# Two-layer kernel with a Hadamard weight stage: first stage of seven gate and up groups on GpSimd, mixer splits placed in the second chunk

## The chip, the cores and the metric

The kernel runs on one core of one Trainium2 chip. The metric is the device time of one execution in microseconds (us). TensorE is called PE below, VectorE DVE, ScalarE ACT, GpSimd POOL, and SyncE, which only issues DMAs here, SP.

## What is computed

Two layers over 2048 tokens of width 512, each with a token mixer and a feed-forward part, all with a residual sum after a layer norm:

```python
x = x + scan_layer(layernorm(x))        # selective scan, 16 states, over time
x = x + ffn(layernorm(x))               # fwht(x*SU_ug), W_up, W_gate, silu, fwht(.*SU_dp), W_down
x = x + mixer(layernorm(x))             # x,z = split(h@W_in.T); x@conv_w.T; (x*D)*silu(z) @ W_out.T
x = x + moe(layernorm(x))               # 64 experts, top 8, capacity 128
```

`fwht` is the Walsh-Hadamard transform. Since it is linear, the kernel applies it to the weights: the transform over the 512 rows of a gate or up weight is a 4 by 4 Hadamard matrix over row blocks of 128, times a 128 by 128 one inside a block. In the mixer the product of `conv_w` and the x half of `W_in` is made once from the weights (the fold). All weights are stored to a scratch tensor in memory as a high and a low part, so that three fast products of rounded numbers stand for one exact one.

## The kernel before

**Tiling and stages.** The 2048 tokens are four chunks of 512. For each chunk the scan runs over 16 states n, and the code divides each state into four positions m = 0 to 3; a position is numbered `state_at(c, n, m)` = 5 + 64c + 4n + m. Every engine walks the same positions in the same order, each with its own program, and does at a position what tables (`prep_at`, `fold_at`, `plain_at`, `quanta_at`) place there. After the four chunks comes a drain, the routing of tokens, and a loop over the 64 experts.

**The scan of a state.** On DVE, state n is: `bx` = u times the broadcast row B_n (L1265), two scans (L1274), two more scans, and `hc` = bx times the broadcast row C_n (L1292); between these DVE does the side work of positions m = 0, 1, 2 and 3. PE makes the broadcasts (`bcast_b` L660, `bcast_c` L668), ACT the decays (L938), and POOL adds `hc` to `y` (L1450, called add(n) below). `bcast_c(n)` waits for hc(n-1); hc(n) waits for `bcast_c(n)` and for add(n-1); in states where the bank of C is lent to other work (`borrowed`), `bcast_c(n)` stands behind the side work of position m = 2.

**The weight stage in chunk 0.** `kinds` = "uduuuduuduud" lists twelve groups, u for 512 columns of the gate or up weight, d for 128 columns of the down weight; group i has four places, 3 + 4i to 6 + 4i, so the stage fills states 0 to 11, one group per state, shifted by two positions. Place (i, m) is on PE four fp32 products (L630, `prep`), on ACT one rounding to the high part at the next position (`prep_hi` L869, L872), on DVE the low part (`prep_lo` L1154, L1159), and on SP two stores (`store_prep`). The raw weights sit in `raw_u`, which has two buffers, and in `raw_d`, which has one. For a d group POOL multiplies the raw block by a scale (L1470) and makes two stages of the transform (L1480, `butterfly`); PE's place (i, 0) of a d group waits for the last of them. The tables put the three parts of the butterfly of the second d group (index g = 1) into states 2, 3 and 4, those of g = 2 at (6,1), (6,3) and (7,1), those of g = 3 at (9,0), (9,1) and (10,0). They are called b(g,0), b(g,1), b(g,2) here.

**The fold and the plain splits.** The fold is eight places, four from position (13,1) of chunk 0 and four from (1,0) of chunk 1. PE multiplies (L642), ACT and DVE split into `fst` (L876, L1166), SP stores. The plain splits are sixteen tiles of `W_in` (z half) and `W_out`, which are only split and stored: SP loads into `praw`, ACT rounds (`plain_hi`, L876), POOL subtracts (`plain_lo`, L1486), SP stores `fst`. `fst` has two buffers; the ACT step of tile i waits for the stores of tile i-2 (`S_ms`). They stand at every third position from (0,2) of chunk 0. The first products of the feed-forward part, read from a ring of six buffers (`load_ring`), start at position (3,0) of chunk 1.

**Queues.** Each engine has one program order, which is also the order of its waits. On POOL, within a position, the side work (`gated_lo`) comes first, then `plain_lo`, then the norm, the corrections of the softplus (L1493, L1495, in states 9 and 10 at m = 3) and the butterflies; add(n) is last in state n.

## Time and profile before

| | us |
|---|---|
| median of 3 runs | 1742.09 (1740.38 to 1750.31) |
| profiled execution | 1734.25 |
| its span on the core | 1732.4 |
| PE busy | 1503.9 (87%) |
| DVE busy | 1062.3 (61%) |
| ACT busy | 586.8 (34%) |
| POOL busy | 794.1 (46%) |
| chunk 0, from bx(0) to bx(0) of chunk 1 | 45.0 to 281.2 |
| chunk 1, likewise | 281.2 to 520.0 |

The page's busy shares are means over stages with different limits. A record of PE includes time in which the next product already runs, so a row of eight products that spans 3.60 us is the better measure of their rate than the mean of one; and each fp32 product of the code is two records. In a timeline row the bracket at the end is the idle time before the row on its engine, and what ended it.

### The profile page before, as it was taken

How to read it: one execution, taken by the hardware profiler on the slowest of the kernel's cores; microseconds unless marked ns; L12 is line 12 of the kernel's file. 1: busy time of each engine (PE TensorE's matmuls, PEld its weight loads, DVE VectorE, ACT ScalarE, POOL GpSimd, SP SyncE). 2: the span in 40 equal slices, each digit the busy share in tenths (PEclk: the TensorE clock that was granted, in tenths of full speed). 3: DMA queues.
4: the chain of work that ended last, by engine and by line, in shares of the span. 5: the costliest groups of instructions: out<-in, count | busy, mean ns of one | idle time of the engine just before them, and what ended most of it. 6: DMA issues, size and time to landing. Idle time of an engine off the chain costs nothing. (4 is left out here: it accounts for less than half of the span.)

```text
span 1732.4 us, 19079 instructions
## 1 busy us (share of the span) xinstructions
PE 1503.9 (87%) x5792; PEld 1032.0 (60%) x5792; DVE 1062.3 (61%) x1591; ACT 586.8 (34%) x1034; POOL 794.1 (46%) x491
## 2 busy tenths in 40 slices
PE   6989966899948899988999899999992799999992
PEld 3344323577736677766887787778772455555551
DVE  4887688787898887889988755452453122222220
ACT  4444633344534335343423322121210122222220
POOL 3467853353644445634554325662276222222222
PEclk9999988999969999999999999999995899999996
DMA  6899663356644666657555568997760699999986
GB/s 203 255 279 279 195 221 130 97 160 196 202 142 149 200 218 219 218 170 245 189 183 167 150 200 275 374 322 233 233 204 25 184 314 312 323 321 322 322 227 126
DMA packets 193541, 380.41 MB, mean 220 GB/s; under 512 B 20994, under 2 KB 95106, under 8 KB 192944
## 3 DMA queue, kind: packets, MB, share of 16 engines
q1 hardware_dynamic: 164784, 321.71, 58.2%
q0 software_dynamic: 20032, 39.92, 9.7%
q10 hardware_dynamic: 8640, 17.73, 2.9%
q8 instruction: 42, 0.69, 0.2%
q14 instruction: 43, 0.35, 0.1%
HBM read 301.65 MB, written 124.35 MB: 246 GB/s over the span
## 5 line engine op out<-in xcount | busy, mean ns | idle before, releaser
L1450 POOL TENSOR_TENSOR y<-y,hc 128x2048 f32<-128x2048 f32 x64 | 293.2, 4581 | 249.0 <-DVE hc L1292 249.0
L588 PE MATMUL bank<-tokT,ring 128*128 128x512 f32 x768 | 307.3, 400 | 12.8 <-DVE xall L1147 6.9
L1274 DVE TENSOR_TENSOR_SCAN bx<-bank,state,bx 128x512 f32<-128x512 f32 x256 | 312.7, 1267 | 0.8
L590 PE MATMUL bank<-tokT,ring 128*128 128x512 f32 x768 | 302.0, 393 | 0.0
L589 PE MATMUL bank<-tokT,ring 128*128 128x512 f32 x768 | 301.7, 393 | 0.0
L938 ACT ACTIVATE bank<-dl,an 128x512 f32<-128x512 f32 x256 | 171.0, 684 | 329.6 <-DVE bx L1274 329.5
L1456 POOL TENSOR_TENSOR act<-th,act 128x512 fp32r<-128x512 f32 x96 | 126.3, 1315 | 269.0 <-ACT act L862 268.7
L817 PE MATMUL bank<-wgu,xeT 128*128 128x384 f32 x512 | 177.7, 490 | 0.0
L588 PEld LDWEIGHTS bank<-tokT,ring 128*128 128x128 f32 x768 | 145.7, 190 | 49.0 <-issue 17.4
L600 PE MATMUL bank<-ring,act 128*128 128x512 f32 x360 | 147.6, 410 | 22.7 <-DVE th L1136 17.4
L590 PEld LDWEIGHTS bank<-tokT,ring 128*128 128x128 f32 x768 | 145.6, 190 | 32.0
L589 PEld LDWEIGHTS bank<-tokT,ring 128*128 128x128 f32 x768 | 145.9, 190 | 29.4
L1292 DVE TENSOR_TENSOR hc<-bx,bank 128x2048 f32<-128x2048 f32 x64 | 146.0, 2282 | 24.4 <-PE bank L668 23.7
L1265 DVE TENSOR_TENSOR bx<-u,bank 128x2048 f32<-128x2048 f32 x64 | 146.0, 2282 | 9.4 <-PE bank L660 6.3
L602 PE MATMUL bank<-ring,act 128*128 128x512 f32 x360 | 143.4, 398 | 0.0
L601 PE MATMUL bank<-ring,act 128*128 128x512 f32 x360 | 143.3, 398 | 0.0
L1532 POOL DMA_INDIRECT slots<-row,idx x128 | 126.2, 986 | 36.9 <-issue 33.5
L1129 DVE SCALAR_TENSOR_TENSOR th<-th,bank 128x512 f32<-128x512 f32 x96 | 65.7, 684 | 100.1 <-ACT th L857 99.9
L817 PEld LDWEIGHTS bank<-wgu,xeT 128*128 128x128 f32 x512 | 93.2, 192 | 52.1 <-issue 2.0
L834 PE MATMUL bank<-wde,hT 96*128 96x512 f32 x256 | 120.6, 593 | 0.5 <-DVE hT L1432 0.5
L1422 DVE SCALAR_TENSOR_TENSOR te<-te,bank 128x192 f32<-128x192 f32 x64 | 22.7, 355 | 156.9 <-ACT te L1078 156.9
L630 PE MATMUL bank<-raw_u,had 128*128 128x512 f32 x256 | 113.7, 594 | 0.2 <-DMA raw_u<-wgT_in 0.2
(147 smaller groups left out, 2032.3 us busy)
## 6 DMA issues: line engine op xcount, KB each, us to landing
ring<-w_all SPq DMA_DIRECT2D x288, 512.0 KB, 3.7
wgu<-wgu_in SPq DMA_DIRECT2D x64, 768.0 KB, 7.6
wde<-wd_in SPq DMA_DIRECT2D x64, 384.0 KB, 6.1
slots<-empty_in SPq DMA_DIRECT2D x16, 1154.0 KB, 8.2
xe<-slots ACTq DMA_DIRECT2D x60, 288.5 KB, 7.1
w_all<-staged_u SPq DMA_DIRECT2D x64, 256.0 KB, 3.2
w_all<-fst SPq DMA_DIRECT2D x48, 256.0 KB, 3.7
w_all<-staged_d SPq DMA_DIRECT2D x32, 256.0 KB, 4.0
```

The lines of the kernel that those rows point to most:

```text
L588: nc.tensor.matmul(b[:, :], w[:, k, 0, :], x[:, 0, k, :], start=(k == 0), stop=False)
L589: nc.tensor.matmul(b[:, :], w[:, k, 0, :], x[:, 1, k, :], start=False, stop=False)
L590: last = nc.tensor.matmul(b[:, :], w[:, k, 1, :], x[:, 0, k, :], start=False, stop=(k == KT - 1))
L600: nc.tensor.matmul(PF[t][:, :], act8[:, 0, j, tok], w[:, 0, :], start=(j == 0), stop=False)
L601: nc.tensor.matmul(PF[t][:, :], act8[:, 0, j, tok], w[:, 1, :], start=False, stop=False)
L602: last = nc.tensor.matmul(PF[t][:, :], act8[:, 1, j, tok], w[:, 0, :], start=False, stop=(j == pairs - 1))
L817: last = nc.tensor.matmul(CG[i % 2][:, 0:2 * FE], xeT[:, i % 2, k, :], wgu[i][:, k, :], start=(k == 0), stop=(k == KT - 1))
L938: nc.scalar.activation(dA[k % 2][:, :], dl[c % 2][:, k, :], ACT.Exp, scale=an[:, k, n:n + 1]).then_inc(S_dA, 1)
L1265: nc.vector.tensor_tensor(bx[:, :, :], u[:, :, :], PB[:, :].unsqueeze(1).to_broadcast([P, KT, CH]), ALU.mult).then_inc(S_bm, 1)
L1274: nc.vector.tensor_tensor_scan(bx[:, k, :], dA[k % 2][:, :], bx[:, k, :], state[:, k, n:n + 1], ALU.mult, ALU.add).then_inc(S_sc, 1)
L1292: nc.vector.tensor_tensor(hc[:, :, :], bx[:, :, :], PC[:, :].unsqueeze(1).to_broadcast([P, KT, CH]), ALU.mult).then_inc(S_cm, 1)
L1450: nc.gpsimd.tensor_tensor(y[c % 2][:, :, :], y[c % 2][:, :, :], hc[:, :, :], ALU.add).then_inc(S_ya, 1)
```

## The change

Three edits. **Pair sums.** For the seven u groups behind the first, POOL makes block 0 + block 2 and block 1 + block 3 (part 0), and the two differences (part 1), into a new buffer `paired`; each part is one instruction of 128 x 1024. PE then needs two products for a place in place of four. Part 0 of group i stands on POOL at the position of place 4i - 2 of the list, which is m = 0 of state i - 1, and part 1 at m = 2 of it. PE waits for the part that it reads (`S_pd`); a part waits for the products that read the same half of `paired` last. **Raw loads.** A buffer of `raw_u` is loaded again after place m = 1 of its group and not after m = 3. **Plain splits.** They stand behind the fold, at every second position from (3,2) of chunk 1 to (11,0), and the numbering of `fst` changes to fit. The sixteen loads and thirty-two stores of SP move with them.

```diff
--- before.py
+++ after.py
@@ -156,6 +156,7 @@
                 raw_d = sb(prep_only, "raw_d", [P, 2, M0 * P])
                 wsdp = sb(prep_only, "wsdp", [P, D])
                 had = sb(prep_only, "had", [P, 2, P])
+                paired = sb(prep_only, "paired", [P, 2, 2, 512])
             rawd, sums = raw_d[:, 0, :], raw_d[:, 1, :]
             ring = sb(A, "ring", [P, RING, 2 * D], f32r)
             expert_buffers((4,))
@@ -209,7 +210,7 @@
             S_x = [sem(f"x_in{c}") for c in range(NCH)]; S_id = sem("identity_in"); S_w = sem("weights_in")
             S_raw = [sem("raw_in0"), sem("raw_in1")]; S_rawd = sem("raw_down_in")
             S_wsc = sem("raw_scaled"); S_pmm = sem("prep_mm"); S_ph = sem("prep_hi"); S_pl = sem("prep_lo")
-            S_bf = sem("butterfly"); S_sel = sem("selectors")
+            S_bf = sem("butterfly"); S_pd = sem("pairs_summed"); S_sel = sem("selectors")
             S_su = [sem(f"up_stored{i}") for i in range(4)]; S_sd = [sem(f"down_stored{i}") for i in range(2)]
             S_wx = sem("winx_in"); S_cv = sem("conv_in"); S_pr = [sem(f"plain_in{i}") for i in range(4)]
             S_fm = sem("fold_mm"); S_mh = sem("mixer_hi"); S_fl = sem("fold_lo"); S_wl = sem("plain_lo")
@@ -272,9 +273,11 @@
             group_of = [kinds[:i].count(kinds[i]) for i in range(len(kinds))]
             prep_places = list(range(3, 3 + 4 * len(kinds)))
             prep_at = {place: (i // 4, i % 4) for i, place in enumerate(prep_places)}
+            u_at = [i for i, kind in enumerate(kinds) if kind == "u"]
+            pairs_at = {prep_places[4 * i - 2 + 2 * part]: (i, part) for i in u_at[1:] for part in range(2)}
             fold_at = {state_at(0, 13, 1) + 3 * m: (0, m) for m in range(KT)} | {state_at(1, 1, 0) + 2 * m: (1, m) for m in range(KT)}
             FOLDS, PLAINS = 2 * KT, 2 * M1
-            plain_at = {state_at(0, 0, 2) + 3 * i: i for i in range(PLAINS)}
+            plain_at = {state_at(1, 3, 2) + 2 * i: i for i in range(PLAINS)}
 
             borrowed_b, borrowed_c = {}, {}
             for c in range(NCH):
@@ -386,16 +389,16 @@
                     def store_mixer(i):
 
                         s = i % 2
-                        if i < M1 or i >= PLAINS:
-                            which = 0 if i < M1 else 1
-                            f = i if i < M1 else i - PLAINS
+                        if i < FOLDS + M1:
+                            which = 1 if i < FOLDS else 0
+                            f = i if i < FOLDS else i - FOLDS
                             m, half = f % KT, f // KT
                             t0 = M0 + 4 * half
                             for part in range(2):
                                 dst = gate_up[which, t0:t0 + 4, :, m, part, :].rearrange("t p c -> p t c")
                                 sp.dma_start(dst, fst[:, s, part, :].rearrange("p (t c) -> p t c", t=4).bitcast(fp32)).then_inc(S_ms[s], 16)
                         else:
-                            j = i - M1
+                            j = i - FOLDS - M1
                             for part in range(2):
                                 sp.dma_start(a["w_all"][3 * (M0 + j) + 2, :, D * part:D * part + D],
                                              fst[:, s, part, :].bitcast(fp32)).then_inc(S_ms[s], 16)
@@ -442,8 +445,11 @@
                             i, m = prep_at[pos - 2]
                             store_prep(i, m)
                             g = group_of[i] + (2 if kinds[i] == "u" else 1)
-                            if m == 3 and g < kinds.count(kinds[i]):
-                                sp.wait_ge(S_pmm, 4 * i + 4)
+                            if m == (1 if kinds[i] == "u" and group_of[i] else 3) and g < kinds.count(kinds[i]):
+                                if kinds[i] == "u" and group_of[i]:
+                                    sp.wait_ge(S_pd, 2 * group_of[i])
+                                else:
+                                    sp.wait_ge(S_pmm, 4 * i + 4)
                                 load_raw(kinds[i], g)
                             if (i, m) == (len(kinds) - 1, 3):
                                 sp.wait_ge(S_pmm, 4 * len(kinds))
@@ -452,7 +458,7 @@
                         if pos - 2 in fold_at:
                             half, m = fold_at[pos - 2]
                             sp.wait_ge(S_fl, KT * half + m + 1)
-                            store_mixer(PLAINS + KT * half + m)
+                            store_mixer(KT * half + m)
                             if half == 0 and m == KT - 1:
                                 load_conv(1)
 
@@ -473,13 +479,13 @@
                                 sp.dma_start(chunk(acc[0], c), xall[:, c]).then_inc(S_x3, 16)
 
                     def plain(pos):
-                        if pos == state_at(0, 0, 0):
+                        if pos == state_at(1, 1, 0):
                             for i in range(4):
                                 load_plain(i)
                         if pos - 3 in plain_at:
                             i = plain_at[pos - 3]
                             sp.wait_ge(S_wl, i + 1)
-                            store_mixer(i)
+                            store_mixer(FOLDS + i)
                             if i + 4 < PLAINS:
                                 load_plain(i + 4)
 
@@ -620,10 +626,19 @@
                     def prep(i, m):
                         g = group_of[i]
                         if kinds[i] == "u":
-                            pe.wait_ge(S_raw[g % 2], 16 * (g // 2 + 1))
+                            if g == 0:
+                                pe.wait_ge(S_raw[0], 16)
+                            else:
+                                pe.wait_ge(S_pd, 2 * (g - 1) + m // 2 + 1)
                         else:
                             pe.wait_ge(S_bf, 4 * g + 4)
                         wait(pe, S_pl, 4 * (i - 1) + m + 1)
+                        if kinds[i] == "u" and g:
+                            for k in range(2):
+                                last = nc.tensor.matmul(PF[m][:, :], had[:, k * (m % 2), :], paired[:, m // 2, k, :],
+                                                        start=(k == 0), stop=(k == 1))
+                            last.then_inc(S_pmm, 1)
+                            return
                         for k in range(4):
                             x = raw_u[:, g % 2, k, :] if kinds[i] == "u" else \
                                 rawd.rearrange("p (x m h) -> p x m h", x=4, m=4)[:, :, k, :]
@@ -877,7 +892,7 @@
 
                     def plain_hi(i):
                         act.wait_ge(S_pr[i % 4], 16 * (i // 4 + 1))
-                        mixer_hi(i, praw[:, i % 4, :])
+                        mixer_hi(FOLDS + i, praw[:, i % 4, :])
 
                     def side(pos):
                         if pos in plain_at:
@@ -887,7 +902,7 @@
                         if pos - 1 in fold_at:
                             half, m = fold_at[pos - 1]
                             act.wait_ge(S_fm, KT * half + m + 1)
-                            mixer_hi(PLAINS + KT * half + m, PF[m][:, :])
+                            mixer_hi(KT * half + m, PF[m][:, :])
                         for h, kind, j in quanta_at.get(pos - 2, ()):
                             if kind == "up":
                                 gated_hi(h, j)
@@ -1161,8 +1176,8 @@
 
                     def fold_lo(half, m):
                         i = KT * half + m
-                        dve.wait_ge(S_mh, PLAINS + i + 1)
-                        dve.wait_ge(S_ms[i % 2], 32 * ((PLAINS + i) // 2))
+                        dve.wait_ge(S_mh, i + 1)
+                        wait(dve, S_ms[i % 2], 32 * (i // 2))
                         nc.vector.tensor_tensor(fst[:, i % 2, 1, :], PF[m][:, :], fst[:, i % 2, 0, :].bitcast(fp32),
                                                 ALU.subtract).then_inc(S_fl, 1)
 
@@ -1480,11 +1495,20 @@
                             nc.gpsimd.tensor_tensor(qv[:, :, i, :], pv[:, :, 0, :], pv[:, :, 1, :], op).then_inc(S_bf, 1)
 
                     def plain_lo(i):
-                        pool.wait_ge(S_mh, i + 1)
+                        pool.wait_ge(S_mh, FOLDS + i + 1)
                         s = i % 2
-                        wait(pool, S_ms[s], 32 * (i // 2))
+                        pool.wait_ge(S_ms[s], 32 * ((FOLDS + i) // 2))
                         nc.gpsimd.tensor_tensor(fst[:, s, 1, :], praw[:, i % 4, :], fst[:, s, 0, :].bitcast(fp32),
                                                 ALU.subtract).then_inc(S_wl, 1)
+
+                    def pair_sums(i, part):
+
+                        g = group_of[i]
+                        pool.wait_ge(S_raw[g % 2], 16 * (g // 2 + 1))
+                        if g > 1:
+                            pool.wait_ge(S_pmm, 4 * u_at[g - 1] + 2 * part + 2)
+                        nc.gpsimd.tensor_tensor(paired[:, part, :, :], raw_u[:, g % 2, 0:2, :], raw_u[:, g % 2, 2:4, :],
+                                                ALU.subtract if part else ALU.add).then_inc(S_pd, 1)
 
                     def correction(c, k):
 
@@ -1505,6 +1529,8 @@
                                 side(state_at(c, n, m))
                                 if state_at(c, n, m) - 1 in plain_at:
                                     plain_lo(plain_at[state_at(c, n, m) - 1])
+                                if state_at(c, n, m) in pairs_at:
+                                    pair_sums(*pairs_at[state_at(c, n, m)])
                                 if c >= 1 and (n, m) == (1, 2):
                                     norm_rstd(pool, n2, c - 1)
                                 if c >= 1 and (n, m) == (14, 0):
```

## Rows read from the trace of the kernel before

**Rows 1.** Groups by shape, 0 to 480 us: busy, mean ns, idle before.
```profile
L630 PE MATMUL bank<-raw_u,had 128*128 128x512 f32 x256 | 113.7, 594 | 0.2 <-DMA raw_u<-wgT_in 0.2
...
L1480 POOL TENSOR_TENSOR raw_d<-raw_d 128x1024 f32<-128x1024 f32 x16 | 37.5, 2365 | 0.2
...
L1486 POOL TENSOR_TENSOR fst<-praw,fst 128x512 fp32r<-128x512 f32 x16 | 20.3, 1270 | 23.4 <-ACT fst L876 23.4
...
L876 ACT ACTIVATE fst<-praw 128x512 fp32r<-128x512 f32 x16 | 9.9, 619 | 0.0
```

**Rows 2.** Windows of states 2, 6, 7 and 10: length, busy by engine, PE clock, DMA.
```profile
core 0: us, PE busy (x) PEld busy (x) DVE busy (x) ACT busy (x) POOL busy (x), PEclk, DMA share, GB/s
...
73.06:86.30 13.24, 13.24 (x34) 5.97 (x33) 11.82 (x11) 5.67 (x10) 10.29 (x4) 1.00 1.06 301
...
133.34:148.26 14.92, 14.92 (x43) 7.28 (x42) 11.93 (x11) 6.87 (x12) 14.92 (x6) 1.00 1.02 294
148.26:165.83 17.57, 17.57 (x43) 7.97 (x42) 12.56 (x12) 7.44 (x13) 11.30 (x6) 1.00 0.86 257
...
196.84:217.58 20.74, 17.67 (x38) 7.41 (x37) 11.98 (x11) 12.19 (x21) 18.89 (x12) 0.92 0.44 132
```

**Rows 3.** Timeline of DVE, chunk 0: start, length, instruction, idle before and releaser.
```profile
79.79 0.75 DVE L1154 SCALAR_TENSOR_TENSOR staged_u<-bank,vec,staged_u 128x512 fp32r<-128x512 f32 x1 [1.42 <-ACT staged_u L869]
...
130.33 2.29 DVE L1292 TENSOR_TENSOR hc<-bx,bank 128x2048 f32<-128x2048 f32 x1 [0.78 <-PE bank L668]
...
163.03 2.29 DVE L1292 TENSOR_TENSOR hc<-bx,bank 128x2048 f32<-128x2048 f32 x1 [1.14 <-PE bank L668]
...
214.77 2.29 DVE L1292 TENSOR_TENSOR hc<-bx,bank 128x2048 f32<-128x2048 f32 x1 [3.28 <-PE bank L668]
```

**Rows 4.** Timeline of PE, chunk 0, the d groups' first places and the fold.
```profile
159.16 3.60 PE L630 MATMUL bank<-raw_d,had 128*128 128x512 f32 x8
162.19 0.80 PE L668 MATMUL bank<-xdr,sel 128*128 128x512 f32 x1
...
209.20 5.31 PE L630 MATMUL bank<-raw_d,had 128*128 128x512 f32 x8 [3.07 <-POOL raw_d L1480]
213.94 0.80 PE L668 MATMUL bank<-xdr,sel 128*128 128x512 f32 x1
...
243.69 8.56 PE L642 MATMUL bank<-conv,winx 128*128 128x512 f32 x16 [3.13 <-DMA winx<-winx_in]
```

**Rows 5.** Windows behind PE's idle time at 206 us, same columns as rows 2.
```profile
209.20:212.20 3.00, 3.00 (x4) 1.45 (x5) 2.10 (x3) 2.76 (x6) 2.92 (x3) 0.50 0.63 176
212.20:215.20 3.00, 3.00 (x8) 1.38 (x8) 0.43 (x1) 0.66 (x2) 2.92 (x3) 0.96 0.61 175
```

**Rows 6.** Timeline of POOL, chunk 0, from hc(5) and from hc(8).
```profile
132.70 4.53 POOL L1450 TENSOR_TENSOR y<-y,hc 128x2048 f32<-128x2048 f32 x1 [10.09 <-DVE hc L1292]
...
138.42 4.52 POOL L1470 TENSOR_TENSOR raw_d<-raw_d,wsdp 128x2048 f32<-128x2048 f32 x1
...
144.12 4.69 POOL L1480 TENSOR_TENSOR raw_d<-raw_d 128x1024 f32<-128x1024 f32 x2
148.78 4.51 POOL L1450 TENSOR_TENSOR y<-y,hc 128x2048 f32<-128x2048 f32 x1
153.25 4.64 POOL L1480 TENSOR_TENSOR raw_d<-raw_d 128x1024 f32<-128x1024 f32 x2
...
178.33 4.54 POOL L1450 TENSOR_TENSOR y<-y,hc 128x2048 f32<-128x2048 f32 x1 [7.17 <-DVE hc L1292]
...
204.49 4.66 POOL L1480 TENSOR_TENSOR raw_d<-raw_d 128x1024 f32<-128x1024 f32 x2
```

**Rows 7.** Timeline of DVE and POOL, chunk 1, states 9 to 11.
```profile
429.77 0.69 DVE L1129 SCALAR_TENSOR_TENSOR th<-th,bank 128x512 f32<-128x512 f32 x1 [5.02 <-ACT th L857]
...
456.31 4.58 POOL L1450 TENSOR_TENSOR y<-y,hc 128x2048 f32<-128x2048 f32 x1
...
461.91 2.28 DVE L1292 TENSOR_TENSOR hc<-bx,bank 128x2048 f32<-128x2048 f32 x1
```

**Rows 8.** The page's DMA issues: count, KB each, us to landing.
```profile
w_all<-fst SPq DMA_DIRECT2D x48, 256.0 KB, 3.7
```

## The prediction

> **What bounds the kernel now.** I read the windows of each scan state in chunk 0, since both edits lie in chunks 0 and 1; then the timeline of DVE, which carries the scan, for what ends each of its waits; then PE and POOL at the places found. The windows show PE full in states 2, 6 and 7, and DVE busy for about 12 us in each [rows 2]. A full PE looks like the bound, but is not in most states: state 2 lasts 13.24 us, which is DVE's 11.8 us and one wait of 1.42 us, ended by ACT's rounding, which stands behind the fourth decay in ACT's program [rows 3]. More speed on PE takes nothing from that. PE ends a wait of DVE by itself in only a few places: 0.78 us at hc(5), 1.14 us at hc(7) [rows 3], about 0.6 us at hc(6), and some 3 us in front of the low parts of states 7 and 9. One wait that looks like PE's is POOL's: hc(10) waits 3.28 us for a broadcast [rows 3], which stands behind the first place of a d group, and this place had waited 3.07 us for POOL's last butterfly [rows 4]. POOL has no idle time in state 6 and 18.9 us of 20.7 in state 10 [rows 2]. So from state 5 to state 10 PE and POOL are nearly level behind DVE, and the change moves work from one to the other.
>
> **Part 1, what PE loses.** Seven groups of four places lose two products each, 56 in all, each of them two records. Eight records take 3.43 us from start to start (the row's 3.60 us less the overlap; the same is seen for u places), or 0.43 us each [rows 4], so PE loses 112 x 0.43 = 48 us of work; the mean of 594 ns in the grouped row would make it 67 us, but that mean counts overlap twice [rows 1]. A u place then takes 1.7 us and a u state 7.5 us of PE. Nearly all of this turns into idle time of PE, for DVE's 13.2 us stay.
>
> **Part 2, what POOL gets.** Fourteen sums of 128 x 1024. The nearest row is the butterfly of the same shape, 2365 ns, from start to start 2.34 us [rows 1, 6]: 33 us more. The sixteen plain subtractions of 1270 ns, 20 us, leave chunk 0 [rows 1]. The net is +13 us on POOL, and what matters is where. Two chains, each from an hc to the last butterfly of a d group, decide.
>
> First chain, from hc(5)'s end. Before: add(5) starts at 132.70, and b(2,2) ends at 157.87 (153.25 and two of 2.3) [rows 6], 25.2 us later, with two plain subtractions of 1.24 us in it. PE came to the place that reads this only at 159.16 [rows 4], 26.5 us after 132.70, and hc(7) could start at 163.03 [rows 3]. After: the two subtractions leave (-2.5), and pair sums (7,0) and (7,1) come in (+4.7), one ahead of b(2,0) and one ahead of b(2,1). The chain is then 27.4 us. No wait sits inside it: hc(6) ends well before add(6) comes up, and the raw blocks land earlier than now. So the place starts 0.9 us later relative to hc(5), although PE by then could have been there some 6 us sooner. And it starts with a cold PE: behind the idle time at 206 us the granted clock was 0.50, the 1.2 GHz level, for 3 us, then 0.96 [rows 5], and the eight records and the broadcast behind them took 4.74 us (209.20 to 213.94) where at the full clock they took 3.03 us (159.16 to 162.19) [rows 4]. That is +1.7 us. Bounds of this one: 0 if the clock stays up, 3.0 us if all eight records run at half speed.
>
> What comes ahead of it: the wait of 0.78 us at hc(5) goes, because the u place before that broadcast is 1.7 us shorter; state 4 loses one plain rounding on ACT that stood ahead of the rounding DVE waits for, 0.6 us [rows 1]; but b(1,2) ends 1.1 us later (the pair sums of states 2 and 3 put add(3) back by that), of which I count 0.7 us at DVE. Net -0.7 us at hc(5). So hc(7) is at -0.7 + 0.9 + 1.7 = +1.9 us.
>
> Second chain, from hc(8)'s end. Before: 178.33 to the end of b(3,2) at 209.15 [rows 6], with two subtractions (2.5 us) and 0.3 us of waiting for a raw block in it. After: pair sums (10,0) and (10,1), +4.7 us. Net +1.9 us; PE starts cold here already before, so nothing is added for the clock. In state 9 DVE would win 0.5 us (PE earlier) and 0.6 us (the rounding gone from ACT), but hc(10) is set by POOL, so both are swallowed. hc(10) stands at 1.9 + 1.9 = **+3.8 us**. States 8 and 11 keep their length: their d places are not changed, and the waits in them are for DVE, ACT and the stores of the two `staged_d` buffers. States 0 to 3 keep theirs as well: pair sums that come late there hold PE, not DVE, for hc needs a place two positions old.
>
> **Part 3, raw loads and DMA in chunk 0.** The earlier reload adds no wait: SP's wait for `S_pd`, with the stores of `staged_u` queued behind it, is met before the low part that SP has just waited for. Leaving out 12 MB of plain traffic relieves a queue that is full in state 2 (share 1.06) and 6 (1.02) [rows 2]. DVE waits for no DMA directly; what can gain is the start of the fold, where PE waits 3.13 us for `winx` [rows 4]. Bounds 0 and -3.1 us; I take -0.5 us, near zero, as the plain stores issued around it are queued behind that load.
>
> **Part 4, plain splits in chunk 1.** Sixteen ACT roundings (0.62 us), sixteen POOL subtractions (1.27 us) [rows 1], 16 loads, 32 stores. All hidden behind 10 us and more per state in which ACT waits for DVE, with these exceptions: at (9,2) ACT is late, DVE waits 5.02 us for its tanh [rows 7], and the rounding stands ahead of it: +0.6 us. In state 10 one subtraction stands ahead of the corrections and add(10): add(10) ends at 460.9 and hc(11) starts at 461.91 [rows 7], a slack of 1.0 us, against 1.27 us: +0.3 us. Each rounding waits for the stores of the tile two before; the spacing of two positions leaves one position (about 3.3 us) between their issue by SP and the wait, where it was three, and the landing takes 3.7 us [rows 8] and SP 1 us for the two. ACT reaches the (n,0) ones about 4.5 us and the (n,2) ones about 7 us behind the issue, by the order of its program, so I count 0, bound 1.5 us a state in eight states. SP's wait for the subtraction has ring loads behind it; the ring holds six loads, so this costs nothing unless SP is late by over 10 us. In sum +0.9 us.
>
> **Sum.** 3.8 - 0.5 + 0.9 = +4.2 us. Against the profiled execution's 1734.25 us that is 1738.4 us; the profiled execution lies 7.8 us under the median of the runs, so against the median of 1742.09 it is **1746.3 us**.
>
> **Rivals.**
> A, the relief of PE counts. If POOL is not late (pair sums cheaper, or PE's arrival the real limit where I see POOL), then hc(5) -0.8, hc(6) -0.6, state 7 about -4.7 (158.3 where hc(7) now starts at 163.03), state 9 -1.1 and part of the 3.3 us at hc(10): -8 to -10 us, 1733 us. For it: PE is full in states 6 and 7. Against it: the row of the same shape on POOL, and POOL's own full state 6 [rows 2, 6].
>
> B, slower by ACT's wait for `fst` in chunk 1. From the point at which a pair of stores takes over some 4.5 us from issue to landing, ACT stands at the plain rounding with the tanh behind it, and DVE waits for that. The price is the excess, 1.5 us in each of eight states, 12 us with both buffers in phase: 1742.1 + 3.3 + 12 = 1757 us. For it: 3.7 us is a median, with ring loads and 1.1 MB fills in the same queue. Against it: the (n,2) tiles have slack, and chunk 1's DMA share is about a half.
>
> C, PE stays cold. PE idles 5 us in most u states after the change. If the clock does not come back within the first d place, then places (8,1) to (8,3), which fill state 8 without slack, take 3.4 us more each: +10 us beyond the sum, 1756 us. For it: the clock stood at 0.50 for 3 us after one idle stretch; against it: it came back at once [rows 5]. The Trainium skill, TensorE: Matmul & The Clock Gate, in "HAM oscillation", says that a kernel whose matmul bursts are parted by idle gaps falls back to the low clock in each gap and pays for the warm-up again each time. By that rule the term of 1.7 us at hc(7) is right and C is its repetition; the trace agrees in one place, with 4.74 against 3.03 us.
>
> D, no effect: the pair sums just fill POOL and DVE hides all, 1742 us. This needs the first chain to end before PE comes, 0.9 us less than I count.
>
> **Chances.** Forecast (between +1 and +8 us) 0.45; D and near it 0.17; A 0.14; B 0.14; C 0.10. A measurement of this kernel can tell about 0.5%, 8.7 us, from no change. Under 1733.4: most of A, 0.13. Above 1750.8: B, C and a little of the forecast's upper end, 0.25. Within: 0.62. The range for 8 in 10 leaves out the outer half of A and the outer part of B and C: 1734 to 1757 us.
>
> **What would show it.** L630 on `raw_u` at 144 records; L630 on `raw_d` at 159 us to start on POOL, with some 6 us of idle time, and at granted clock 0.5; hc(7) to wait about 6 us for L668; bx(8) about 1.9 us and bx(11) about 3.8 us later than 165.83 and 217.58; PE busy in chunk 0 down by 50 us or more; chunk 1 within 1 us of its 238.7 us. I am wrong if hc(7) starts before 163 us (then A), if ACT's L876 waits for the stores of `fst` in chunk 1 (then B), or if the windows of states 8 and 9 show the clock near 0.5 (then C).

## The result, and the profile after

| | before, on the same chip | after |
|---|---|---|
| median (lowest to highest) | 1745.13 (1740.38 to 1750.31) | 1776.84 (1770.84 to 1781.55) |
| profiled execution | 1734.25 | 1777.88 |
| span | 1732.4 | 1776.0 |
| chunk 0, bx(0) to bx(0) of chunk 1 | 236.3 | 241.7 |
| chunk 1, likewise | 238.7 | 259.1 |

The ratio is 1.0173, 95% interval 1.0144 to 1.0202. The forecast, 1746.3 with 1734 to 1757 as its range, is wrong. The change costs 31.7 us by the medians. The two profiled executions lie 43.6 us apart, since that of before is 10.9 us under its median and that of after 1.0 us above. To find where the time went, I took the start of `bx` of every state from both traces. The last state of chunk 3 starts 29.4 us later: +5.6 at the end of chunk 0, +20.4 in chunk 1, +3.4 in chunks 2 and 3. The other 14.2 of the 43.6 us lie behind that state. That stretch is the same program in all kernels here and took 751.5 us (before) to 765.7 us (after) in the thirteen traces, and 761.9 in that of before with idle products, which has nothing of the change; so I don't count it to the change. Of the executions behind the medians below, one of the twelve of "five groups, idle products" took 5800.27 us at a mean granted clock of 0.258; its median counts it, its ratio does not.

First the line of busy times on the page of after. POOL was at 794.1 us before and PE at 1503.9.

```profile
PE 1482.6 (83%) x5680; PEld 1019.6 (57%) x5680; DVE 1063.4 (60%) x1591; ACT 587.0 (33%) x1034; POOL 826.3 (47%) x505
```

PE has the 112 records less that were counted, and POOL the 14 more. Then the groups by form of the first 520 us of after (busy us and mean ns, then idle us ahead of them and what ended most of it), to hold against [rows 1].

```profile
L638 PE MATMUL bank<-paired,had 128*128 128x512 f32 x112 | 59.3, 660 | 24.7 <-POOL paired L1510 24.7
L1510 POOL TENSOR_TENSOR paired<-raw_u 128x1024 f32<-128x1024 f32 x14 | 32.9, 2359 | 0.0
L891 ACT ACTIVATE fst<-praw 128x512 fp32r<-128x512 f32 x16 | 10.0, 626 | 40.7 <-DMA w_all<-fst 40.6
```

The pair sum costs 2359 ns, as the butterfly of the same shape did. The third line is the result: sixteen roundings of 626 ns, and ahead of them ACT stood idle for 40.6 us waiting for stores of `fst`. Now the windows of chunk 0, chunk 1, and two of 3 us at the first place of the second last d group (start:end and length, busy us of each engine, granted clock, DMA share, GB/s).

```profile
45.20:286.89 241.69, 172.76 (x378) 73.97 (x376) 188.74 (x158) 101.50 (x172) 158.55 (x57) 0.89 0.60 179
286.89:545.94 259.05, 206.43 (x762) 147.44 (x763) 200.58 (x182) 108.19 (x185) 130.79 (x67) 0.88 0.61 192
160.16:163.16 3.00, 3.00 (x4) 1.45 (x5) 0.00 (x0) 0.00 (x0) 0.00 (x0) 0.51 0.62 173
163.16:166.16 3.00, 3.00 (x8) 1.35 (x8) 0.33 (x1) 0.57 (x1) 0.00 (x0) 0.92 0.00 0
```

In chunk 1 DVE, which carries the scan, is busy for 200.6 of 259.1 us, against 199.0 of 238.7 before. Its work has hardly grown; its waits have.

**Chunk 1.** The view of waits of after, in 287 to 546 us (us in total, times, longest):

```profile
ACT fst L891 <- DMA w_all<-fst: 40.6, 7, 11.3
DVE th L1144 <- ACT th L872: 32.9, 10, 8.6
```

and of before, in 281 to 520 us:

```profile
DVE th L1129 <- ACT th L857: 16.0, 6, 5.3
```

DVE's waits for the tanh grew by 16.9 us, and this is most of the chunk's 20.4. One place shows the mechanism, the rounding of plain tile 10, which needs the buffer of tile 8. Timelines of after around 420 us, SP, then POOL (the low part of tile 8), ACT (the rounding of tile 10 and the tanh) and DVE (start, us, engine, line, in brackets the idle time and what ended it):

```profile
410.73 0.98 SPq L399 DMA_DIRECT2D w_all<-fst  x2
413.57 5.76 SPq L425 DMA_DIRECT2D ring<-w_all  x3
419.38 0.64 SPq L414 DMA_DIRECT2D slots<-empty_in  x1
420.07 1.10 SPq L403 DMA_DIRECT2D w_all<-fst  x2
```

```profile
409.10 1.30 POOL L1501 TENSOR_TENSOR fst<-praw,fst 128x512 fp32r<-128x512 f32 x1 [5.23 <-ACT fst L891]
```

```profile
429.97 0.63 ACT L891 ACTIVATE fst<-praw 128x512 fp32r<-128x512 f32 x1 [11.32 <-DMA w_all<-fst]
430.50 0.67 ACT L872 ACTIVATE th<-bank,gsh 128x512 f32<-128x512 f32 x1
```

```profile
431.21 0.69 DVE L1144 SCALAR_TENSOR_TENSOR th<-th,bank 128x512 f32<-128x512 f32 x1 [8.60 <-ACT th L872]
```

POOL ends the low part of tile 8 at 410.4. SP first issues the stores of tile 7 (410.73), three ring loads, for which it waits for PE, and a fill of 1154 KB; the pair of tile 8 it issues at 420.07, 9.7 us behind the low part. ACT came to the rounding at 418.65 (429.97 less 11.32 us of waiting), so 1.4 us before the stores were even issued, and gets the buffer back at 429.97, 8.8 us behind the end of the issue and 9.9 behind its start. The tanh of L872 is next in ACT's program, and DVE is idle for 8.60 us until it has it. The other six waits have the same two parts: SP issues 1.3 to 9.2 us behind the low part, and ACT has the buffer 5.4 to 9.8 us behind the issue. The DMA view of 410 to 432 us says what the stores were among (count, KB each, median us from issue to landing):

```profile
q1 hardware_dynamic: 3175, 6.27, 94.0%
w_all<-fst SPq DMA_DIRECT2D x7, 256.0 KB, 7.8
slots<-empty_in SPq DMA_DIRECT2D x1, 1154.0 KB, 9.7
```

The queue takes 94.0% of sixteen engines' time in this stretch, and a store lands after 7.8 us, where the median over the whole kernel of before was 3.7 [rows 8]. In the kernel before, the same work with its fill, but without the plain tiles, took 69.9% (405 to 427 us):

```profile
q1 hardware_dynamic: 1535, 4.85, 69.9%
```

**Chunk 0.** DVE's timeline at hc(7) and hc(10) of after, to hold against [rows 3]:

```profile
165.83 2.29 DVE L1307 TENSOR_TENSOR hc<-bx,bank 128x2048 f32<-128x2048 f32 x1 [6.62 <-PE bank L683]
...
219.96 2.29 DVE L1307 TENSOR_TENSOR hc<-bx,bank 128x2048 f32<-128x2048 f32 x1 [6.77 <-PE bank L683]
```

PE's, to hold against [rows 4]:

```profile
160.16 5.40 PE L645 MATMUL bank<-raw_d,had 128*128 128x512 f32 x8 [4.87 <-POOL raw_d L1495]
164.99 0.80 PE L683 MATMUL bank<-xdr,sel 128*128 128x512 f32 x1
...
213.77 5.91 PE L645 MATMUL bank<-raw_d,had 128*128 128x512 f32 x8 [5.97 <-POOL raw_d L1495]
219.12 0.80 PE L683 MATMUL bank<-xdr,sel 128*128 128x512 f32 x1
```

And POOL's, the first chain, to hold against [rows 6]:

```profile
132.75 4.54 POOL L1465 TENSOR_TENSOR y<-y,hc 128x2048 f32<-128x2048 f32 x1 [6.22 <-DVE hc L1307]
137.25 2.34 POOL L1510 TENSOR_TENSOR paired<-raw_u 128x1024 f32<-128x1024 f32 x1
139.55 4.54 POOL L1485 TENSOR_TENSOR raw_d<-raw_d,wsdp 128x2048 f32<-128x2048 f32 x1
144.03 2.38 POOL L1510 TENSOR_TENSOR paired<-raw_u 128x1024 f32<-128x1024 f32 x1
146.35 4.69 POOL L1495 TENSOR_TENSOR raw_d<-raw_d 128x1024 f32<-128x1024 f32 x2
150.98 4.53 POOL L1465 TENSOR_TENSOR y<-y,hc 128x2048 f32<-128x2048 f32 x1
155.44 4.66 POOL L1495 TENSOR_TENSOR raw_d<-raw_d 128x1024 f32<-128x1024 f32 x2
```

From 132.75 to 160.1 POOL has no gap. PE waited 4.87 us for the last butterfly, and then its clock stood at 0.51, the 1.2 GHz level, for 3 us, before it was 0.92 (the windows above). The eight records and the start of the broadcast took 4.83 us, where they took 3.03 us at the full clock [rows 4].

### The profile page after: what moved, and what is told of

Same layout as the page of the kernel before. It is cut to its first block and busy times, and to the rows that moved or that the text cites. A ratio compares the mean times of both kernels' runs of the same rounds, so it can differ in the third digit from the quotient of the medians.

```text
span 1776.0 us, 18881 instructions
## 1 busy us (share of the span) xinstructions
PE 1482.6 (83%) x5680; PEld 1019.6 (57%) x5680; DVE 1063.4 (60%) x1591; ACT 587.0 (33%) x1034; POOL 826.3 (47%) x505
## 5 line engine op out<-in xcount | busy, mean ns | idle before, releaser
L1592 POOL DMA_INDIRECT out<-ye,tok x32 | 49.3, 1541 | 141.2 <-ACT ye L1100 124.1
```

## The experiments

The theory after this result: chunk 1 is lost to ACT's wait for the stores of `fst`, which land late for two reasons, a queue shared with ring loads and fills, and an SP that comes to the stores late; chunk 0 is lost to POOL's two chains and PE's low clock behind each. The rivals: chunk 1 is lost because the added ACT and POOL work is itself too much there; the two parts of the change need each other; the pair sums are slow at all seven groups, not in the two chains. Each table row below gives how much later (us) than in the trace of before a state's `bx` starts. A row is one execution. After, fills later, and fills later with early stores run the same code in chunk 0 and differ there by up to 0.4 us, so I read nothing into less than that; the execution of five groups is the slowest of its ten, 9.4 us above its median.

| kernel | (0,5) | (0,8) | (0,11) | (1,0) | (1,7) | (1,11) | (2,0) | (3,15) |
|---|---|---|---|---|---|---|---|---|
| after | 1.0 | 2.8 | 5.2 | 5.6 | 9.9 | 24.0 | 26.0 | 29.4 |
| pairs only | 5.4 | 9.6 | 15.0 | 15.7 | 15.9 | 15.9 | 15.9 | 19.2 |
| plains only | 0.2 | 0.5 | -0.5 | -0.2 | 4.1 | 17.2 | 17.5 | 20.9 |
| four `fst` | 2.2 | 4.0 | 6.4 | 6.9 | 7.6 | 8.1 | 10.1 | 10.6 |
| fills later | 1.0 | 2.8 | 5.2 | 5.5 | 8.4 | 14.5 | 16.7 | 22.6 |
| fills later, stores early | 1.4 | 3.2 | 5.6 | 5.9 | 6.4 | 7.8 | 10.1 | 16.3 |
| five groups | 1.2 | -2.1 | -1.9 | -1.4 | 2.5 | 3.0 | 3.3 | 9.1 |
| idle products | 0.5 | -0.4 | 2.3 | 2.8 | 3.5 | 4.0 | 5.9 | 7.2 |
| sums on DVE | 0.2 | 3.3 | 4.3 | 6.0 | 10.0 | 10.5 | 10.8 | 10.9 |
| five groups, plains back | 4.9 | 2.9 | 2.8 | 3.1 | 3.0 | 3.0 | 3.0 | 3.1 |
| five groups, idle products | 0.2 | -3.8 | -6.5 | -6.3 | -6.0 | -5.4 | -5.1 | -2.6 |
| before with idle products | 0.4 | -0.8 | -2.8 | -2.5 | -2.4 | -2.4 | -2.4 | -2.0 |

Before had a median of 1745.13 beside after; of 1737.26 beside pairs only, plains only, four `fst` and fills later; of 1742.41 beside five groups, idle products, sums on DVE, and five groups with the plains back; and of 1737.28 beside the other three.

### One part of the change at a time

**Pair sums alone.** The plain splits stay at their old places in chunk 0. From after:

```diff
-            plain_at = {state_at(1, 3, 2) + 2 * i: i for i in range(PLAINS)}
+            plain_at = {state_at(0, 0, 2) + 3 * i: i for i in range(PLAINS)}
```

> The pair sums and the earlier raw loads alone; the plain splits stay in chunk 0 as before. Theory now (two parts: POOL's chains in chunk 0 cost about 5 us, ACT's waits for the stores of fst in chunk 1 cost about 20 us): with the plain subtractions still on POOL, each of the two chains is 2.5 us longer than in the changed kernel, so chunk 0 ends 9 to 10 us later than in the kernel before, chunks 1 to 3 keep the lengths of before, and the time is before + 8 to 11 us. Rival (it is the pair sums that disturb what comes later, through POOL and the reads of raw blocks): chunk 1 is longer by 10 us or more here too, and the time is before + 25 us or more.

Measured: 1756.20 us, ratio 1.0087 (1.0048 to 1.0126). Chunk 1 lost 0.2 us, chunk 0 lost 15.7. The chains account for what was expected, but 5.4 us are gone already at state 5, which no theory had. Of these, 4.5 are lost in state 3. POOL and DVE at its end in this run, then in the kernel before:

```profile
104.45 4.54 POOL L1465 TENSOR_TENSOR y<-y,hc 128x2048 f32<-128x2048 f32 x1
104.59 4.48 DVE L1132 TENSOR_SCALAR n_ngt<-n_mvt 128x4 f32<-128x4 f32 x1
```

```profile
99.08 4.53 POOL L1450 TENSOR_TENSOR y<-y,hc 128x2048 f32<-128x2048 f32 x1 [1.63 <-DVE hc L1292]
102.56 1.08 DVE L1117 TENSOR_SCALAR n_ngt<-n_mvt 128x4 f32<-128x4 f32 x1
```

POOL is full in states 2 and 3 with plain subtractions and pair sums together, and add(3) starts at 104.45 in place of 99.08. DVE pays for that in two ways. A u place comes late on PE, and DVE waits 1.0 us for its rounding. The other 3.4 us are in a tiny instruction of the layer norm, `n_ngt` (128 x 4), which takes 0.17 us where POOL is idle (570.03 us in after). It took 1.08 us before, 1.94 after and 4.48 here, and each time it ended within 0.1 us of the end of POOL's add(3): it stood until POOL's instruction was done. So POOL can take the plain subtractions or the pair sums, but not both in chunk 0; moving the plain splits saves 10.1 us there (15.7 against 5.6).

**Plain splits moved, alone.** From after, the four products of each place, the old raw waits, and no pair sums:

```diff
-            pairs_at = {prep_places[4 * i - 2 + 2 * part]: (i, part) for i in u_at[1:] for part in range(2)}
+            pairs_at = {}
```

> The move of the plain splits alone; PE keeps four products for each place. Theory: chunk 0 is 1 to 3 us shorter than before (the ACT roundings are gone from DVE's way, PE still sets hc(7)), chunk 1 is 18 to 22 us longer, with ACT's L891-kind wait for the stores of fst at about 40 us in sum; time before + 17 to 23 us. Rival (the two parts disturb each other): chunk 1 is longer by less than 10 us here.

Measured: 1760.68 us, ratio 1.0133 (1.0092 to 1.0174); chunk 0 -0.2 us, chunk 1 +17.7. The view of waits of chunk 1 of this run:

```profile
ACT fst L878 <- DMA w_all<-fst: 38.8, 7, 9.7
```

Chunk 1's loss comes with the plain splits and needs nothing of the pair sums. The freed time in chunk 0, expected to give 1 to 3 us, is worth nothing to a kernel without pair sums.

### What makes the stores late

**Four buffers of `fst`.** The same work, in four buffers in place of two, so that ACT's step of tile i waits for the stores of tile i-4.

```diff
-                fst = sb(split_only, "fst", [P, 2, 2, 512], f32r)
+                fst = sb(split_only, "fst", [P, 4, 2, 512], f32r)
...
-                        wait(act, S_ms[i % 2], 32 * (i // 2))
-                        nc.scalar.activation(fst[:, i % 2, 0, :], src, ACT.Copy).then_inc(S_mh, 1)
+                        wait(act, *stored(i))
+                        nc.scalar.activation(fst[:, i % 4, 0, :], src, ACT.Copy).then_inc(S_mh, 1)
```

> The changed kernel with four buffers of fst in place of two, so that a rounding waits for the stores of the tile four before. Theory (the wait for the stores is the whole of chunk 1's loss): ACT's wait for those stores falls from 40 us to under 5 us, chunk 1 is within 3 us of its length before (238.7 us), chunk 0 stays at + 5 us, and the time is before + 5 to + 10 us. Rival (DMA load of the plain tiles slows the ring, or POOL and ACT simply have too much in chunk 1): the wait is gone, but chunk 1 stays 10 us or more longer.

Measured: 1752.35 us, ratio 1.0082 (1.0058 to 1.0106). ACT waits for no store of `fst` in chunk 1 any more, and DVE's waits for the tanh are down from 32.9 to

```profile
DVE th L1146 <- ACT th L874: 17.4, 8, 5.5
```

Chunk 1 costs 3.2 us in place of 20.4. So 17 us of it were the wait, and 3.2 us are what is left with the added work of ACT and POOL. The rival that this work is the whole loss falls. The medians agree: the kernel is 15.1 us slower than before (5 to 10 were expected) in place of 31.7. Of the 3.2 us, 1.3 are `n_ngt` again, in state 3: a plain subtraction of 1.30 us stands ahead of POOL's add(3), and `n_ngt` takes 2.95 us until that add ends, where it took 1.71. State 12, which has no plain tile, is 1.6 us longer at a granted clock of 0.86 in place of 1.00, and state 2 is 1.7 shorter at 0.99 in place of 0.91, so these two cancel. (Chunk 0 is 1.3 us worse than in after, 0.9 of it in state 1; why stays open.)

**Fills later.** The sixteen fills of 1.15 MB, which began in chunk 1, all go to chunk 2.

```diff
-                        if state_at(1, 8, 0) <= pos < state_at(3, 0, 0) and (pos - state_at(1, 8, 0)) % 6 == 0:
+                        if state_at(2, 0, 0) <= pos < state_at(3, 0, 0) and (pos - state_at(2, 0, 0)) % 4 == 0:
```

> The changed kernel with the sixteen fills of the slots (1.15 MB each) all in chunk 2, at every fourth position, none in chunk 1. It tells apart why the stores of fst land late. If it is the fills ahead of them in the DMA queue: the waits of 11.3 and 8.0 us in states 8 and 10 of chunk 1 fall to 3 us or less, chunk 1 gets about 10 to 13 us shorter than in the changed kernel, and the time is before + 17 to 22 us. If it is the late issue by SP behind the ring loads: the waits stay above 6 us each, and the time stays at before + 28 to 33 us.

Measured: 1762.60 us, ratio 1.0147 (1.0106 to 1.0189). Chunk 1 costs 11.2 us (16.7 less the 5.5 of chunk 0), so 9.2 us are gone. The view of waits of chunk 1:

```profile
ACT fst L891 <- DMA w_all<-fst: 27.6, 6, 7.4
```

Neither expectation held. The fills are about one half of the loss; something else makes the other. At tile 10 the buffer now came back 5.5 us behind the issue in place of 9.9, but SP still issued the stores 10.1 us behind the low part.

**Fills later, and the stores issued a position earlier.** SP looked at a plain tile three positions behind it, behind the ring loads of the positions between, each of which waits for PE.

```diff
-                        if pos - 3 in plain_at:
-                            i = plain_at[pos - 3]
+                        if pos - 2 in plain_at:
+                            i = plain_at[pos - 2]
```

> The changed kernel with all fills in chunk 2 and the stores of a plain tile issued by SP one position earlier. Chunk 1 was 20.3 us longer than before in the changed kernel and 11.1 us with the fills away. If the rest is the late issue behind ring loads that wait for PE: the waits for the stores of fst in states 6 to 8 fall to under 3 us each, and chunk 1 is 3 to 6 us longer than before, as with four buffers. If it is the time that the DMA queue takes: chunk 1 stays 9 to 11 us longer.

Measured: 1752.64 us, ratio 1.0077 (1.0054 to 1.0100). Chunk 1 costs 4.2 us, 7.0 less than with the fills moved alone, as expected of a late issue, though two waits stayed above 3 us. At the five waits SP issues 0.0 to 6.1 us behind the low part, where the same stores had 1.3 to 10.1, and the time from issue to buffer is 4.8 to 6.5 us, as with the fills moved alone (5.3 to 6.4). The view of waits:

```profile
ACT fst L891 <- DMA w_all<-fst: 13.6, 5, 4.5
```

13.6 us of waiting are left on ACT, and hardly any of them reach DVE, since the chunk is 1.0 us from what four buffers give. The split of chunk 1's 20.4 us is then: 9.2 the fills, 7.0 SP's late issue, 1.0 the rest of the round trip, 3.2 what four buffers leave. The order in which the causes are taken away matters to such a split; the reverse order was not run. What the plain tiles themselves add to the queue's load was not tested apart.

### What the two chains cost, and PE's clock

**Five groups.** From here on with four `fst`. Groups 7 and 10, whose pair sums stand in the two chains, keep the four products.

```diff
+            paired_at = [i for i in u_at[1:] if i not in (7, 10)]
+            pairs_at = {prep_places[4 * i - 2 + 2 * part]: (i, part) for i in paired_at for part in range(2)}
```

> The kernel with four buffers of fst, and pair sums for five groups only: groups 7 and 10 of the list, whose sums stand in POOL's two chains, keep four products on PE. Theory (chunk 0 loses by the 4.7 us of pair sums in each chain and by the cold start of PE behind it): hc(7) starts near 160 us (163.0 before, 165.8 changed), bx(11) comes 4 to 6 us earlier than before (5.2 us later in the changed kernel), chunk 1 stays 3 us longer; time before - 4 to + 1 us. Rival (PE's spare time is what counts, and fewer pair sums take it away): hc(7) and bx(11) stay later than before, time before + 5 us or more.

Measured: 1745.12 us, ratio 1.0013 (0.9994 to 1.0031), 2.7 us above before by the medians. bx(8) is 2.1 us ahead of before and 6.1 ahead of four `fst` alone: the first chain is the pair sums of group 7 and what they set off. At hc(10) the gain expected did not come. PE's timeline:

```profile
206.25 6.32 PE L648 MATMUL bank<-raw_d,had 128*128 128x512 f32 x8 [5.49 <-POOL raw_d L1498]
212.01 0.79 PE L686 MATMUL bank<-xdr,sel 128*128 128x512 f32 x1
```

The place is free at 206.25, but PE had idled for 5.49 us, and the eight records up to the broadcast took 5.76 us, against 3.03 at the full clock [rows 4].

**Idle products ahead of the wait.** All seven groups, four `fst`, and work added that is not of the reference: six products with no use for their result, in the bank that the place itself is to fill, ahead of PE's wait for the butterfly, at three d groups.

```diff
+                            if m == 0 and g:
+                                for k in range(6):
+                                    nc.tensor.matmul(PF[m][:, :], had[:, 0, :], wsdp[:, :], start=True, stop=True)
                             pe.wait_ge(S_bf, 4 * g + 4)
```

> The kernel with four buffers of fst, and twelve records of idle products (six products of constants into a bank that is free then) in front of the wait for the butterfly at the first place of the second to fourth d groups. Extra work, output the same. If the cold start of PE behind its idle time is 1.7 us on the path at hc(7) and at hc(10) each: the granted clock there stays near 1, the broadcast follows the place's start by 3.0 us and not by 4.8 us, chunk 0 is 3 to 4 us shorter than with four buffers alone, time before + 8 to + 12 us. If the clock has no part: chunk 0 stays as it is, or longer by what the idle products overrun.

Measured: 1745.73 us, ratio 1.0023 (1.0004 to 1.0041). PE's timeline at hc(7):

```profile
151.90 5.31 PE L639 MATMUL bank<-wsdp,had 128*128 128x512 f32 x12
158.66 3.70 PE L651 MATMUL bank<-raw_d,had 128*128 128x512 f32 x8 [1.45 <-POOL raw_d L1501]
161.79 0.80 PE L689 MATMUL bank<-xdr,sel 128*128 128x512 f32 x1
```

The place and the start of its broadcast take 3.13 us and not 4.83: the 1.7 us of the low clock are shown, at the size that the sum had. Against the kernel with four `fst`, bx(6) gains 2.7 us, bx(8) 4.4 us in all, and chunk 0 as a whole 4.1. At hc(10) the products came late and ran past the butterfly's end:

```profile
207.36 6.02 PE L639 MATMUL bank<-wsdp,had 128*128 128x512 f32 x12
213.22 3.17 PE L651 MATMUL bank<-raw_d,had 128*128 128x512 f32 x7
```

The place starts at 213.22 there, and what the clock gave back was spent on waiting for the idle products.

**The four sums of groups 7 and 10 on DVE.**

```diff
+                            for part in range(2):
+                                dve.wait_ge(S_pmm, 4 * u_at[g - 1] + 2 * part + 2)
+                                nc.vector.tensor_tensor(paired[:, part, :, :], raw_u[:, g % 2, 0:2, :], raw_u[:, g % 2, 2:4, :],
+                                                        ALU.subtract if part else ALU.add).then_inc(S_wx, 1)
```

> The kernel with four buffers of fst and seven groups, but the four pair sums of groups 7 and 10 on DVE, at the second position of states 6 and 9. POOL's chains lose 4.7 us each, DVE gets about 2.4 us (4 sums of 1.1 to 1.2 us) in each of the two states. Theory: hc(7) starts near 161 us, bx(11) is 3 to 5 us earlier than before, chunk 1 3 us longer, time before - 3 to + 2 us. Rival (DVE is the bound and pays each of its own sums in full): chunk 0 is no shorter than in the kernel before, time before + 3 us or more.

Measured: 1753.88 us, ratio 1.0074 (1.0050 to 1.0097). The expectation failed on the price of a sum. DVE's timeline and POOL's:

```profile
140.59 5.57 DVE L1198 TENSOR_TENSOR paired<-raw_u 128x1024 f32<-128x1024 f32 x2
...
192.85 6.42 DVE L1198 TENSOR_TENSOR paired<-raw_u 128x1024 f32<-128x1024 f32 x2
```

```profile
137.29 4.50 POOL L1498 TENSOR_TENSOR raw_d<-raw_d,wsdp 128x2048 f32<-128x2048 f32 x1 [1.04 <-DMA raw_d<-wdT_in]
141.87 6.50 POOL L1508 TENSOR_TENSOR raw_d<-raw_d 128x1024 f32<-128x1024 f32 x2
```

Two sums take 5.57 and 6.42 us on DVE where about 2.3 were expected (an estimate: half of 2.28 us for 128 x 2048, twice), and the two butterflies of POOL beside the first pair 6.50 us where they took 4.69 [rows 6]. The records fit with the two engines taking turns: POOL's multiplication ends at 141.79, and from there a sum of 1.15, a butterfly of 2.33, a sum and a butterfly make 148.75, where the last one ended at 148.37. The Trainium skill, GPSIMD Engine Reference, section 1, says that GpSimd's SBUF interfaces are shared with VectorE, with contention for DVE instructions that have two SBUF inputs; this run agrees, and adds the price to both.

**Five groups, plain splits back in chunk 0, two `fst`.** Parts as in the first experiment and in five groups.

```diff
-            plain_at = {state_at(1, 3, 2) + 2 * i: i for i in range(PLAINS)}
+            plain_at = {state_at(0, 0, 2) + 3 * i: i for i in range(PLAINS)}
+            paired_at = [i for i in u_at[1:] if i not in (7, 10)]
```

> Pair sums for the same five groups, and the plain splits left in chunk 0 with two buffers of fst. Theory: the two chains are as long as before the change (25.2 and 30.8 us), so hc(7) and hc(10) come at the times of before or 1 us earlier; but POOL's states 2 and 3 hold pair sums and plain splits, which cost 4.4 us in the run with the pair sums alone, and this stays; chunk 1 as before; time before + 2 to + 6 us. If the plain splits in chunk 0 were not what cost there: time before - 1 to + 1 us.

Measured: 1748.50 us, ratio 1.0040 (1.0019 to 1.0061), +6.1 by the medians and +3.1 at the end of the chunks. Again 4.9 us are lost by state 5 and none in chunk 1. POOL is as full as in the first experiment: the last butterfly of the second d group ends at 114.3 us, where it ended at 109.8 before. Here `n_ngt` took only 0.40 us, as it came just ahead of add(3), and the loss is in state 4 instead, where DVE waits 4.68 us for ACT's rounding of the first d place, which PE began 4.6 us later. So this is the first part of what the pair sums alone cost, without the two chains.

**Five groups with idle products.** Four `fst`; six idle products at the first of the later d groups, five at the last, in which PE waits longest.

```diff
+                            for k in range({1: 6, 3: 5}.get(g, 0) if m == 0 else 0):
+                                nc.tensor.matmul(PF[m][:, :], had[:, 0, :], wsdp[:, :], start=True, stop=True)
```

> The kernel with pair sums for five groups and four buffers of fst, with idle products (six and five of constants) in front of the butterfly waits of the second and the fourth d group. Extra work, output the same. If the cold start costs what the run with idle products showed (1.7 to 2.7 us for each start): bx(8) comes 4 to 5 us and bx(11) 5 to 7 us earlier than in the kernel before, chunk 1 is 4 to 5 us longer as in the run with five groups, and the time is before - 4 to + 1 us.

Measured: 1738.88 us, ratio 1.0000 (0.9985 to 1.0015). PE's timeline at hc(10), which now starts at the full clock:

```profile
204.32 3.70 PE L651 MATMUL bank<-raw_d,had 128*128 128x512 f32 x8 [1.01 <-POOL raw_d L1501]
207.46 0.80 PE L689 MATMUL bank<-xdr,sel 128*128 128x512 f32 x1
```

3.14 us in place of 5.76. bx(11) is 6.5 us ahead of before, the best of all kernels here. Chunk 1 then takes 1.2 us of it back and chunks 2 and 3 another 2.5, and by the medians nothing is won (1738.88 against 1737.28).

**Before with idle products.** Nothing of the change; four idle products at the first of these d groups, three at the last.

```diff
+                            for k in range({1: 4, 3: 3}.get(g, 0) if m == 0 else 0):
+                                nc.tensor.matmul(PF[m][:, :], had[:, 0, :], wsdp[:, :], start=True, stop=True)
```

> The kernel before, with idle products (four and three) in front of the butterfly waits of the second and the fourth d group, where PE idles 4.2 and 3.1 us and starts cold. Extra work, output the same, nothing of the change in it. If the cold start is on the path in the kernel before: hc(5) comes up to 0.8 us and hc(10) 1.7 to 2.5 us earlier, the rest keeps its length, time before - 1 to - 4 us. If the clock has no part in it: no difference beyond 0.5 us in chunk 0.

Measured: 1737.69 us, ratio 0.9992 (0.9976 to 1.0009). The chunks end 2.0 us earlier, which the medians cannot tell from no change. At bx(11) it is 2.8 us ahead, against 6.5 with the five groups, so 3.7 us there come from the five groups' pair sums and the plain splits moved out of the chains, with PE's clock kept. Which of the two it is was not separated.

## Why the prediction was wrong

**The step that failed** is in part 4: "I count 0, bound 1.5 us a state in eight states" for ACT's wait on the stores of `fst`. It measured 17.2 us, the difference of chunk 1 between two and four buffers (20.4 - 3.2). Three things in its working were off. The landing was taken at 3.7 us [rows 8], a median over the whole kernel; behind ring loads and a fill of 1154 KB it was 7.8 us in the median, and 8.8 to 9.9 at the worst place. ACT was taken to come to the rounding 4.5 or 7 us behind the issue; at the seven waits it came between 2.7 us ahead of the issue and 7.1 behind it, three times ahead, since SP reached the stores late, behind ring loads that wait for PE. Issuing them one position earlier was worth 7.0 us. And the bound was no bound: it took an excess of 1.5 us once a state, where seven waits of 2 to 11 us came out.

**Rival B was the right mechanism**, with its place, and was given 0.14. The point of 4.5 us "from issue to landing" was passed: 7.8 us in the median of the stretch shown. Its price of 12 us was too low by 5, for the same reasons. What spoke against it, "the (n,2) tiles have slack, and chunk 1's DMA share is about a half", did not hold: the share over the chunk went from 0.50 to 0.61 with the plain tiles, and it is 94.0% in the stretch in which the tile stands, where it was 69.9% already before. And two of the seven waits were of (n,2) tiles, 8 and 10, the longest, of 11.3 us, among them.

**The rest of part 4** was too low: four buffers leave 3.2 us, forecast 0.9. The missing term is DVE's `n_ngt` in state 3, 1.3 us, which stands until POOL's add ends.

**The first chain was right.** Forecast 27.4 us from add(5) to the last butterfly; from 132.75 to 160.1 it was 27.3. **The clock was right**: forecast 4.74 us for the place and broadcast behind the wait, measured 4.83, and idle products took 1.7 us out of it. hc(7) lies 2.8 us later than before, forecast 1.9. The difference is ahead of the chain: the net -0.7 us at hc(5) did not come. The wait of 0.78 us [rows 3] did go, but bx(5) was already 1.0 us late, and add(5) started at 132.75, where it had started at 132.70. Of that 1.0 us, 0.9 were lost in state 3, of which the prediction said that it keeps its length: add(3) was late by the pair sums, and `n_ngt` stood until its end, 1.94 us in place of 1.08. State 4 kept its length. The place then began 1.0 us later (160.16, and 159.16 before [rows 4]), and 1.8 us went to the clock.

**The second chain was forecast 0.5 us too short.** hc(10) is 5.2 us later (219.96, and 214.77 before [rows 3]), forecast 3.8: 0.9 of the difference is from hc(7), and 2.4 in place of 1.9 from there to hc(10), where the eight records and the broadcast took 5.35 us, against 4.74 before, behind a longer idle time (5.97 us against 3.07 [rows 4]).

**Part 3's gain of 0.5 us did not come.** The traffic that left chunk 0 gave nothing to the fold; chunk 0 loses another 0.4 us behind bx(11).

**Rival A** falls with the chain. PE did lose work, though busy time in chunk 0 fell only by 29.5 us, from 202.3, where 50 were forecast: a record of the places that are left took 660 ns in the mean, with the clock low in more stretches (0.89 for the chunk, 0.94 before). Nothing came of what was freed; PE idled 24.7 us ahead of the products on `paired`. **Rival C** falls too: the clock was back at 0.92 within 3 us, and bx(9) was 2.8 us late as bx(8) was. **Rival D** is refuted by the chain.

**Chunks 2 and 3** lost 3.4 us, and nothing of the change stands there. Among the kernels this term goes from 0.1 us (sums on DVE, and five groups with the plains back) to 6.2 (fills later, stores early). The traces show what it is made of. In chunks 2 and 3 the states have the same lengths in all thirteen traces to about 0.4 us, except for a few in which PE's clock was low in some and not in others, and what follows on these. State 12 of chunk 2, before and after:

```profile
704.29:714.85 10.56, 10.33 (x45) 8.55 (x46) 9.38 (x7) 6.96 (x8) 6.01 (x3) 1.00 0.51 158
730.11:742.22 12.11, 11.88 (x45) 9.72 (x46) 9.37 (x8) 7.90 (x9) 7.51 (x3) 0.85 0.50 142
```

It takes 10.6 us at a granted clock of 1.00 and 12.1 to 13.3 us at 0.77 to 0.85; state 2 of chunk 3 takes 14.7 and, at 0.89, 15.9 to 16.3. In after the two cost 3.0 of the 3.4 us. The kernel before has such a state too: state 12 of chunk 3 took 12.16 us at 0.86, and 10.54 to 10.58 at 1.00 in three others. What makes the clock fall in one kernel and not in another stays open; each kernel has one trace.

## What to carry to other kernels

When a step with a buffer of its own is moved, its round trip is what has to be costed again: the landing time in the stretch where it will stand, behind what the queue carries there, and the moment at which the issuing queue really gets to the store, not its position in the order. An engine with spare busy time is no place for work if its instructions stand in a chain that ends in another engine's wait; count the chain from the event that starts it, and look for small instructions of another engine that end only with this one's. Where an engine waits long enough to lose its clock, a few idle products can hold it, but only so many as end ahead of the wait.

## What the runs showed of the hardware

- A store of 256 KB landed after 3.7 us in the median of the kernel before, 7.8 us in a stretch of after in which the queue took 94.0% of the engines' time.
- PE behind an idle time of 3.1 to 6.0 us runs its next eight records and the start of a broadcast in 4.7 to 5.8 us, where it took 3.0 to 3.1 us behind 0 to 1.5 us; idle products ahead of the wait give back 1.7 us at one place and 2.6 at another, and nothing where they run past the event waited for.
- DVE and POOL, each with two SBUF inputs, ran as if they took turns: sums of 128 x 1024 took 2.8 and 3.2 us on DVE, where 1.15 were estimated, and POOL's butterflies beside the first pair 3.25 us where they took 2.35.
- DVE's `n_ngt`, 128 x 4, took 0.17 us with POOL idle. Beside POOL's add of 4.5 us it took 1.08, 1.94 and 4.48 us, each time until that add ended (103.6, 104.6 and 109.0 us).
